# Attention of a pair moved from behind the query projection to before it on TensorE, in a two-layer linear-attention kernel

## What is computed

```python
xn = layernorm(x)
q, k, v = xn @ Wq + bq, xn @ Wk + bk, xn @ Wv + bv      # masked k and v
q = softmax(q.reshape(T, heads, dh), axis=-1)
k = softmax(k.reshape(T, heads, dh), axis=0)            # over the tokens
attn = einsum('nhd,nhl->hdl', k, v)                     # per head, dh x dh
y = einsum('nhd,hdl->nhl', q, attn).reshape(T, D)
scale, shift = split(silu(emb) @ W_emb + b_emb)
h = silu(layernorm(y) * (1 + scale) + shift) @ W_out + b_out
x = x + h
```

## Time and profile before

| quantity | before |
|---|---|
| median of three timed runs | 858.48 us |
| the profiled execution's own time | 857.14 us |
| span of the instructions in it | 855.1 us |
| outside the span in that execution | 2.0 us |
| TensorE matmul busy | 838.2 us, 98% of the span |
| VectorE, ScalarE, GpSimd busy | 679.3, 603.1, 548.9 us |
| mean granted TensorE clock | 1.00 of full speed |

### The profile page before, as it was taken

The page is one execution under the profiler, slowest core; times in us unless marked ns, Lnnn a source line. Parts: engine busy times, 40 slices in busy tenths (PEclk is TensorE's granted clock), DMA queues, the critical chain, the costliest instruction groups (busy, mean ns, idle before and its releaser), DMA issues.

```text
span 855.1 us, 20095 instructions
## 1 busy us (share of the span) xinstructions
PE 838.2 (98%) x6659; PEld 719.9 (84%) x6659; DVE 679.3 (79%) x1362; ACT 603.1 (71%) x1442; POOL 548.9 (64%) x741
## 2 busy tenths in 40 slices
PE   7999999999999999999999999999999999999998
PEld 7778888888888888888878888888888888888886
DVE  6987778778788788778887887787788787787766
ACT  5376687686676776686876886776776686676665
POOL 3467766766766666766767667667667666765641
PEclk9999999999999999999999999999999999999999
DMA  8876676766667756555587556656566656566441
GB/s 309 286 225 201 201 218 199 228 216 205 195 210 208 233 197 199 179 165 175 169 247 233 185 172 200 201 180 201 179 204 201 202 186 189 178 194 211 142 160 62
DMA packets 139404, 169.81 MB, mean 199 GB/s; under 512 B 12302, under 2 KB 112006, under 8 KB 139302
## 3 DMA queue, kind: packets, MB, share of 16 engines
q1 hardware_dynamic: 138512, 167.56, 62.5%
q10 hardware_dynamic: 790, 0.98, 0.4%
HBM read 95.61 MB, written 72.88 MB: 197 GB/s over the span
## 4 chain that ended last, share of the span: by engine, by line
PE 83%; DMA 6%; DVE 4%; issue 2%; SPq 2%; POOL 1%; ACT 1%; DVEq 0%; POOLq 0%; ACTq 0%
PE PS L1152 72%; PE PS L1248 6%; PE PS L1232 3%; DMA X<-in_x 2%; DMA XT<-x_turned 1%; DMA x_turned<-XS 1%; DMA k_turned<-KT 1%; DMA QT<-qy_turned 1%; POOL XL L667 0%; SPq L400 0%; PE PS L1322 0%; DMA EK<-k_turned 0%; DVE BNX L1515 0%; PE PS L1276 0%; PE PS L1291 0%
## 5 line engine op out<-in xcount | busy, mean ns | idle before, releaser
L680 POOL TENSOR_TENSOR HL<-H,HH 128x512 fp32r<-128x512 f32 x60 | 77.5, 1292 | 185.3 <-ACT HH L916 185.3
L867 ACT ACTIVATE Z<-QT,FC,FA 128x128 f32<-128x128 f32 x240 | 99.0, 483 | 87.7 <-DMA QT<-qy_turned 87.7
L1152 PE MATMUL PS<-XH,WH_k 128*128 128x256 f32 x512 | 149.8, 293 | 0.7 <-DVE KN L1581 0.7
L1152 PE MATMUL PS<-XL,WH_k 128*128 128x256 f32 x512 | 144.8, 283 | 0.0
L1152 PE MATMUL PS<-XH,WL_k 128*128 128x256 f32 x512 | 144.8, 283 | 0.0
L953 ACT ACTIVATE XN<-X,NBX,RSX 128x512 f32<-128x512 f32 x60 | 48.8, 813 | 85.5 <-POOL NBX L629 85.5
L829 ACT ACTIVATE SK<-SK,KN 128x128 f32<-128x128 f32 x256 | 98.9, 387 | 10.7 <-DVE KN L1581 10.4
L1152 PE MATMUL PS<-WH_o,HH 128*128 128x512 f32 x248 | 101.3, 408 | 2.0 <-issue 1.9
L1152 PE MATMUL PS<-WH_v,XH 128*128 128x512 f32 x256 | 100.8, 394 | 0.0
L1152 PE MATMUL PS<-WH_q,XH 128*128 128x512 f32 x256 | 100.7, 393 | 0.0
L1152 PE MATMUL PS<-WL_v,XH 128*128 128x512 f32 x256 | 100.3, 392 | 0.0
(11 more groups left out here) (171 smaller groups left out, 2106.6 us busy)
## 6 DMA issues: line engine op xcount, KB each, us to landing
qy_turned<-QS SPq DMA_DIRECT2D x60, 512.0 KB, 2.9
QT<-qy_turned SPq DMA_DIRECT2D x240, 128.0 KB, 3.1
EK<-k_turned SPq DMA_DIRECT2D x128, 128.0 KB, 2.8
x_turned<-XS SPq DMA_DIRECT2D x30, 512.0 KB, 3.3
XT<-x_turned SPq DMA_DIRECT2D x120, 128.0 KB, 3.5
k_turned<-KT SPq DMA_DIRECT2D x52, 256.0 KB, 3.8
out_x<-X SPq DMA_DIRECT2D x31, 256.0 KB, 3.2
X<-in_x SPq DMA_DIRECT2D x11, 512.0 KB, 5.3
```

What stands on the lines that cost most here:

```text
L680: eng.tensor_tensor(hl_of(o), h_of(o), hh_of(o).bitcast(F32), ALU.subtract).then_inc(pool_hl, 1)
L867: z = eng.activation(z_of(o)[:, c * P:c * P + P].rearrange("p (q n) -> p q n", q=Q), src, ACT.Identity, bias=FC[l][:, c, b:b + 1], scale=F ...
L1152: mm = eng.matmul(dst, left[a](c), right[b](c), start=(c == 0 and a + b == 0), stop=(c == C - 1 and a == 1))
```

## The change

In `step(s)` of TensorE's list, the loop that calls `attention(j)` for the tiles of `attention_at(s)` stands before `queries(s)`, in place of after it (and after `conditioning_fold`, which stands in odd steps only). It is called for s = 5 to 30 and s = 37 to 61. The parts written by hand, the other engines' lists, all semaphores and all buffers stay as they are, and no instruction is added or removed.

```diff
                 values(s)
                 if s in FILM_SLOTS:
                     conditioning(FILM_SLOTS.index(s))
+                for j in attention_at(s):
+                    attention(j)
                 queries(s)
                 if s in FILM_SLOTS:
                     conditioning_fold(FILM_SLOTS.index(s))
-                for j in attention_at(s):
-                    attention(j)
                 output(s - 4)
                 mix(s - 2)
```

## The result

The changed kernel takes 894.28 us (891.5 to 896.36, four runs) against 859.01 us, a ratio of 1.0399 with a 95% interval of 1.0374 to 1.0424. The forecast was 890.4 us in a range of 873 to 905. The profiled execution has a span of 889.6 us where the one before had 855.1: 34.5 us more, forecast 31.9.

A forecast was written before the change was run, and what follows sets the result against it. TensorE was taken to bound the kernel: 855.1 us of span plus 31.9 of key waits gives 887.0, 889.0 with 2.0 outside the span, and 890.4 with 1.3 for the timed median; range 873 to 905.

The forecast's parts named there:

- What bounds the kernel: TensorE, busy in all but 1.7 us of the steady stretches; a new wait on it is paid in full.
- How much earlier, and the slack of each pair: Attention is asked for 2.73 us earlier; keys' slacks in 25 steady pairs are 0.03 to 3.61 us, two above 2.73.
- The sum: Over 23 steady pairs, 2.73 us less each slack gives 30.7 us, plus 1.2 for release: 31.9 us.
- The prediction's sign: TensorE's waits show a new row, attention on the key DMA, some 23 times, 28 to 32 us total, none over 3.
- 1.2 us for the release: TensorE starts 0.05 us after the keys land, in each of 23 waiting pairs.
- No payment for the next: The keys' chain is tied to the odd step's queries on TensorE, so each pair pays its wait anew.
- the bound of 11 us: Most that could be gained if `KT` on VectorE no longer waits for GpSimd, 0 to 0.49 us a pair; taken as 0.
- Edits at nothing: Later queries of even steps, `output` waiting for `HL`, SyncE's queue and the change of layer: all put at 0 us.
- Early transfers: Rival 1: the key transfers come early enough with the waits, so 857 to 861 us at best; chance 0.04.
- the 2 us of the rule set against the rows: The skill's DMA rule makes the key chain 2 us shorter, so the sum falls from 32 to 2 us.
- The rival of the clock: Rival 4: half clock behind each TensorE wait costs 6.4 us, 147 for 23: 1037 us; chance 0.08 with rival 3.
- a clock row below 1.00: Sign of being wrong: TensorE's granted clock, 1.00 in both steady stretches before, falls.

The follow-up runs named there:

- the kernel without the wait: Changed kernel, but in steady steps the key reads take the previous pair's keys, so they don't wait for the write: 860.91 us beside 858.25 for the kernel before.
- the fillers: Purposeless matmuls ahead of the attention: four in 20 even steps of the changed kernel, 893.01 us; twelve in even steps with attention ahead of `values`, 969.7 us.

## Why the prediction was right

**What bounds the kernel** held: a new wait on TensorE is paid nearly in full. That 34.5 us of waits in steady steps stand against 34.5 us more of span is in part luck: TensorE's idle time has grown by 32.1 us, as some other waits shrank (the prediction's 1.7 us of idle in the steady stretches nearly all went), and its busy time by 2.4, most of it the clock.

**How much earlier, and the slack of each pair** held. The two pairs that were to cost nothing cost nothing, 23 wait, and the longest wait is 2.7 us, as the sum had it for the tightest pair (which is now another one: the waits vary from run to run, with the write's 2.8 to 5.0 us).

**The sum** was 31.9 us, in the trace it is 34.5; the second profile of the same kernel has 33.7 us in 24 waits, of which 1.9 by hand, so 31.8. The term was sized to within what two executions differ by. The prediction's sign was 28 to 32 us of waits in total, and the two profiles have 36.1 and 33.7, so that bound was too narrow. In its 1.2 us for the release, the 0.03 us of the tightest pair is no sign of a release, as TensorE didn't wait there.

**No payment for the next** held: the chain from `SQ` to the reads is 6.17 us before and 6.18 after. GpSimd's lateness did shrink, from 0.49 to 0.25 us in the pair shown, and was worth at most 0.1 us a pair (from `SQ` to the write's issue the mean is 2.53 us before and 2.47 after): the bound of 11 us was far too wide, the value taken, 0, about right. Nothing came back at the change of layer beyond the 0.6 us by which its two waits are shorter.

**Edits at nothing** held: no other row of TensorE's waits has grown by more than a microsecond, and the kernel without the wait stands at 860.9 us, 2.7 above the one beside it, where 0 was put: a small cost of the order may be missing in the sum.

**The rivals.** Early transfers did not happen: the write takes what it took. (Done pair by pair, the 9 us of that rival come to 8, and the 2 us of the rule set against the rows to less than 1; neither changes the forecast.) The rival of the clock was half right, though I gave it a small chance for a large price. The prediction named a clock row below 1.00 as a sign that it was wrong, and the second stretch has 0.99: on this point it was. The falls exist, but one to a few in a run, each about 1.5 us and not 6.4, as the clock is back before the queries are through. My argument against it, that a wait of 2.8 us in the kernel before had left the clock at 1.00, was one case, and one case doesn't carry it: of two waits of nearly one length, one has a fall behind it and the other none. This term is missing in the sum. Its size is an estimate: the mean clocks of the four runs average 0.993, those of the kernel before 0.998, and the difference, 0.005 of 893 us, is some 5 us at most (0 to 8 in the single runs); how many of these falls lie in the start-up, and what they cost there, isn't known. It can account for the 4 us by which the median stands above the forecast, though how much of them exactly the fillers left open. With the attention ahead of `values` the waits are 2.8 times as long in total, up to 5.4 us each, and busy time grew by 46 of 142 us. The Trainium skill's "TensorE: Matmul & The Clock Gate", section "Why this matters for your kernels", which warns of idle gaps between bursts of matmuls, was nearer than I weighed it; the traces agree in so far as each fall in a steady step stands behind such a gap, of 1.87 to 2.83 us in the two profiles of the changed kernel.

## What to carry to other kernels

On an engine that is always busy, the distance between a request and its data is what a block of work covers; before moving a consumer forward, read in each step how long the data had been there, subtract the length of the block it is moved past, and add up what is below zero. Means hide it: here slacks of 0.03 to 3.6 us gave waits from none to 2.7 us, and half of the move cost a ninth of the whole. And look at the neighbours on both sides: what the block moves away from loses its cover as well, as the kernel with the attention one projection later shows.

## What the runs showed of the hardware

In two traces of the changed kernel TensorE's clock fell from 2.4 to 1.2 GHz behind waits of 1.87, 2.48 and 2.83 us, each time at a price of some 1.5 us, and didn't behind others of 2.62, 2.70 and 2.71 us. With 27 waits of up to 5.4 us the mean clock of the run was 0.940, and 2.8 us of matmuls without a purpose in each wait of a steady step made that kernel 30 us faster, at a mean clock of 0.984 to 0.988.
